# A sparse FFN layer's expert rows: scattered to their places block by block, and loaded plainly at the end

## The chip, the cores and the metric

One core of one Trainium2 chip. The metric is the device time of one execution of the whole program in microseconds (us), the median of several runs. Engines: PE (TensorE), DVE (VectorE), ACT (ScalarE), POOL (GpSimd), SP (SyncE, which issues most DMAs here).

## The reference

The program has four attention layers and four FFN layers over x of 8 batches x 112 tokens x 256. The change lies in the sixth step, a mixture of experts:

```python
logits = CAP * tanh((xn @ wg.T) / CAP)             # xn: normalized x, 896 tokens x 256; 8 experts
probs = softmax(logits)
topk_vals, topk_ids = top_k(probs, 2)
topk_w = topk_vals / sum(topk_vals)
h = gelu(xn @ w1[e].T) * (xn @ w3[e].T)            # 1024 wide, per chosen expert e
out[t] = sum over the 2 choices of topk_w * (h @ w2[e].T)
x = x + tanh(g_ffn[2]) * out
```

With the inputs given, the 1792 choices fall on the eight experts as 318, 226, 200, 56, 234, 127, 338 and 293.

## The kernel before, in words

`sparse_ffn` sorts the 1792 (choice, token) pairs into 21 blocks of 128 slots, each block of one expert. An expert's pairs fill 3, 2, 2, 1, 2, 1, 3 and 3 blocks here, so blocks 0 to 16 hold rows and 17 to 20 are empty; an empty slot counts as token 0 for the gather.

`Assignment` makes the routing: DVE works out choices, counts and the slot of every pair (`vector`, L1870 to L1980); PE turns this into lists of token numbers per block by products with one-hot matrices (`tensor_lists`, L1845, into `psT`), and into the weights of the last two blocks (`tensor_weights`, `psW`). All 896 normalized rows are stored to memory (`rows_dram`, L2090), since indirect DMAs read from there.

Then the blocks k = 0 to 20, each engine running through them in its own written order, tied by semaphores:
- **POOL** `gather(k)` (L2111 to L2118): an indirect DMA fetches the 128 rows of block k into one of two buffers. From k = 2 it waits until PE has transposed block k-2 (`x_turned`). POOL also makes two iota tiles (`spread`, L2132) for the last two blocks.
- **PE** `turn(k)` transposes the rows (L2154). ACT and DVE split them and the weights into high and low parts. `up(k, j)` (L93 to L95) makes half j of both up products; `turn_hidden` (L2177) transposes the gated hidden rows; `down(k)` (L2190) makes the block's output `psY`. A loop pass k issues up(k,0), turn_hidden(2k-1), turn(k+1), up(k,1), down(k-1), turn_hidden(2k).
- **DVE** `move(k)` (L2311) copies `psY` to one of two buffers `ys`; it waits until the store two blocks earlier is done.
- **SP** loads the weights (L2072, L2079), 3 MB a block, through a ring of three blocks, and issues `store(k)` (L2084): 128 rows of `ys` go to `y_dram` in slot order. The store of block k-4 stands in pass k of SP's loop, for blocks 0 to 18.

The last two blocks (LATE = 2) come back another way. Their slots in `y_dram` are filled with zeros early (L2092). ACT copies their outputs to `ys` (`move_late`, L2259), and PE multiplies them by `spread`, a 0/weight matrix of slots by tokens, into four PSUM banks `back`, two batches in each (L2219).

At the end POOL, once all nineteen stores have landed, issues sixteen indirect gathers (L2142), one per batch and choice, that fetch each token's row from its slot. DVE adds both choices with their weights to x (`gathered(b)`, L2318), then the `back` rows (`returned(b)`, L2324), then the statistics for the next layer's norm (L128, L138, L108). DVE's order is gathered(0), gathered(1), and then for each b gathered(b+2), returned(b), statistics of b-1. A barrier and the next layer follow.

Of the kernel before, what the change touches and what calls it, by code (L numbers as in the profile page):

```python
# [5 lines left out]
ALU = mybir.AluOpType  # L6
# [7 lines left out]
P = 128  # L14
# [1713 lines left out]
class Assignment:  # L1728
# [6 lines left out]
    def __init__(self, m, st, xT, wgT, ps, size, blocks, late, gate=6):  # L1735
# [40 lines left out]
        self.slot_index = m.sb("r_slot_index", [T, 2 * B], I32)  # L1776
        self.passed, self.expert_f = m.sb("r_passed", [1, blocks, E - 1]), m.sb("r_expert_f", [1, blocks])
        self.expert = m.sb("r_expert", [1, blocks], I32)
        self.lists = m.sb("r_lists", [T, 2 * B, 2, blocks], BF16)
# [4 lines left out]
        self.psT = ps[:, 256:256 + size // P * 2 * blocks]  # L1784
# [13 lines left out]
    def gpsimd(self, pool):  # L1798
# [14 lines left out]
        pool.memset(self.ones, 1.0).then_inc(s, 1)  # L1813
        pool.memset(self.sel[:, B, :], 0.0).then_inc(s, 1)
# [6 lines left out]
    CONSTS = 13  # L1821
# [23 lines left out]
    def tensor_lists(self, pe):  # L1845

        W = 2 * self.blocks
        for h in range(self.size // P):
            for n in range(2 * B):
                pe.wait_ge(self.s_hot_made, n + 1)  # L1850
                mm = pe.matmul(self.psT[:, h * W:(h + 1) * W], self.hot[:, n, P * h:P * h + P],
                               self.lists[:, n].rearrange("t s k -> t (s k)"), start=(n == 0), stop=(n == 2 * B - 1))
        mm.then_inc(self.s_listed, 1)
# [16 lines left out]
    def vector(self, dve):  # L1870
# [75 lines left out]
        dve.tensor_copy(self.slot_index, self.slot).then_inc(self.s_slot_made, 1)  # L1946
# [9 lines left out]
        stepped(dve.tensor_scalar(self.lists[:, :, 1, :], self.inside, self.t_at, None, ALU.mult))  # L1956
        settle()
# [4 lines left out]
        stepped(dve.tensor_reduce(self.token_f, self.psT.rearrange("p (h s k) -> p h k s", s=2, k=K), AX, ALU.add))  # L1962
# [15 lines left out]
        dve.wait_ge(self.s_weights_listed, 1)  # L1978
        dve.tensor_reduce(self.slot_weight, self.psW.rearrange("p (j h) -> p h j", j=3), AX, ALU.add
# [3 lines left out]
def sparse_ffn(nc, st, xT, io):  # L1983
# [17 lines left out]
    y_dram = nc.dram_tensor("f2_y", (BLOCKS * SIZE, D), F32).ap()  # L2001
    with ExitStack() as ctx:
# [61 lines left out]
        def _(sp):  # L2064
# [17 lines left out]
            def store(k):  # L2082
                sp.wait_ge(y_moved, k + 1)
                sp.dma_start(y_dram[k * SIZE:(k + 1) * SIZE, :], ys[k % 2]).then_inc(y_stored[k % 2], 16)  # L2084

# [5 lines left out]
            sp.wait_ge(zeroed, 1)  # L2091
            sp.dma_start(y_dram[(BLOCKS - LATE) * SIZE:BLOCKS * SIZE, :].rearrange("(h p) d -> p h d", p=P),  # L2092
                         bass.AP(tensor=zeros.tensor, offset=zeros.offset,
                                 ap=[list(zeros.ap[0]), [0, LATE], list(zeros.ap[1])])).then_inc(zeros_stored, 16)
# [3 lines left out]
            for k in range(1, BLOCKS):  # L2098
                e = sp.value_load(routing.expert[0:1, k:k + 1], min_val=0, max_val=E - 1)
                load_up(k, e)  # L2100
                if k > 1:
                    load_down(k - 1, last)
                last = e
                if 3 < k and k - 4 < BLOCKS - LATE:
                    store(k - 4)
            load_down(BLOCKS - 1, last)
            for k in range(BLOCKS - 4, BLOCKS - LATE):
                store(k)

        @block.gpsimd  # L2110
        def _(pool):  # L2111
            def gather(k):
                if k > 1:
# [4 lines left out]
                                        ).then_inc(rows_loaded[k % 2], 16)  # L2118

# [669 lines left out]
```

## Time and profile before

| | us |
|---|---|
| median of 3 runs | 1308.14 |
| lowest, highest | 1308.1, 1309.41 |
| the profiled execution, its own time | 1311.16 |
| its span, first to last instruction | 1309.4 |
| blocks of the sparse layer, from the first up product to the last down product's copy | 804.0 to 1029.6 |

The profiled execution is one execution; all rows below are of it, and their times count from the span's start. "busy" is the time in which an engine works; `PEclk` is the share of TensorE's clock that was granted. `[idle before <-releaser]` is the time for which the engine stood idle ahead of a row and what ended it; "remote" is a semaphore's rise for which the profile has no instruction. PE's rows of one kind are merged, and the ends of matmuls are modelled.

### The profile page before, as it was taken

To read this page: it belongs to the slowest core of one execution; us is meant where nothing else is said; L and a number is where in the kernel's file an instruction comes from. 1 tells how busy PE (TensorE), PEld (TensorE's weight loads), DVE (VectorE), ACT (ScalarE), POOL (GpSimd) and SP (SyncE) were. 2 spreads that over 40 slices of the span, in tenths; PEclk is the share of its full clock that TensorE was granted. 3 is DMA by queue.
4 is the path that set the end of the run, shared out by engine and by line. 5 is a ranking of instruction groups with operands and counts; after the bars stand their busy time and mean duration, and the time that the engine had idled before them with its cause. 6 is when DMAs were issued, how large, how long until landed. Compare 5 with 4: busy or idle time off the path is not lost. (4 is left out here: it accounts for less than half of the span.)

```text
span 1309.4 us, 23700 instructions
## 1 busy us (share of the span) xinstructions
PE 1157.5 (88%) x8549; PEld 880.4 (67%) x8549; DVE 817.3 (62%) x1967; ACT 660.4 (50%) x1536; POOL 513.0 (39%) x527
## 2 busy tenths in 40 slices
PE   3999999999999769658999965999999489999877
PEld 3677777777777436545777754888888367777544
DVE  6665555645544443575778756766665377777686
ACT  3345554445554313225667633665664057766565
POOL 1455554555555200028888772000101341361132
PEclk9999999999999879787999976999999779999997
DMA  6000000000000124030010044999993160000000
GB/s 192 2 12 13 8 6 13 1 13 1 1 1 1 34 76 138 24 96 23 24 46 25 12 133 158 376 377 379 350 343 125 51 191 24 14 14 2 2 8 22
DMA packets 81459, 109.03 MB, mean 83 GB/s; under 512 B 9664, under 2 KB 57168, under 8 KB 81344
## 3 DMA queue, kind: packets, MB, share of 16 engines
q1 hardware_dynamic: 79568, 102.93, 24.4%
q0 software_dynamic: 1776, 4.59, 1.2%
q8 instruction: 70, 1.15, 0.4%
q14 instruction: 45, 0.37, 0.1%
HBM read 102.91 MB, written 4.59 MB: 82 GB/s over the span
## 5 line engine op out<-in xcount | busy, mean ns | idle before, releaser
L907 POOL TENSOR_SCALAR a_arena<-a_arena 112x487 f32<-112x487 f32 x128 | 192.7, 1517 | 176.9 <-DVE a_arena L1124 176.9
L1213 ACT ACTIVATE a_arena<-banks,a_arena 112x487 f32<-112x487 f32 x128 | 84.2, 663 | 192.0 <-DVE a_arena L1118 192.0
L1118 DVE TENSOR_REDUCE a_arena<-banks 112x2 f32<-112x974 f32 x64 | 75.0, 1172 | 101.5 <-PE banks L995 101.5
L397 POOL TENSOR_TENSOR a_arena<-a_arena 112x375 f32<-112x375 f32 x128 | 114.5, 920 | 24.4 <-ACT a_arena L704 24.1
L513 PE MATMUL banks<-ident,a_arena 112*126 112x112 f32 x768 | 106.2, 275 | 12.9 <-POOL a_arena L397 10.7
L513 PEld LDWEIGHTS banks<-ident,a_arena 112*126 112x126 f32 x768 | 77.9, 144 | 47.2 <-issue 27.1
L2060 DVE TENSOR_TENSOR f_up_low<-f_arena,f_up_high 128x1024 fp32r<-128x1024 f32 x80 | 95.7, 1218 | 9.5 <-ACT f_up_high L2232 9.5
L712 ACT COPY a_arena<-banks 126x336 f32<-126x336 f32 x128 | 56.0, 437 | 72.7 <-PE banks L513 72.7
L2232 ACT CAST f_up_high<-f_arena 128x1024 fp32r<-128x1024 f32 x84 | 84.2, 1055 | 8.3 <-DMA f_arena<-in_L_ffn_w1T 7.8
L93 PE MATMUL banks<-a_wv_high,a_kvT_high 128*122 128x512 f32 (+1 forms) x224 | 86.3, 385 | 2.1 <-DVE a_kT_low L1070 2.1
L2116 POOL DMA_INDIRECT f_arena<-f_rows,f_arena x21 | 20.2, 961 | 171.0 <-PE banks L2154 156.7
L93 PE MATMUL banks<-a_kvT_high,a_wk_high 128*128 128x488 f32 (+1 forms) x192 | 82.7, 431 | 4.3 <-DVE a_wk_low L1086 3.1
L2190 PE MATMUL banks<-f_arena 128*128 128x256 f32 x336 | 77.7, 385 | 4.2 <-ACT f_arena L2252 4.2
L704 ACT ACTIVATE a_arena<-a_arena 112x375 f32<-112x375 f32 x128 | 76.9, 605 | 2.8 <-DVE a_arena L620 2.8
L94 PE MATMUL banks<-a_wv_low,a_kvT_high 128*122 128x512 f32 (+1 forms) x224 | 78.0, 348 | 0.0
L95 PE MATMUL banks<-a_wv_high,a_kvT_low 128*122 128x512 f32 (+1 forms) x224 | 77.9, 348 | 0.0
L704 ACT ACTIVATE a_arena<-banks,a_arena 112x375 f32<-112x375 f32 x128 | 72.8, 579 | 9.3 <-DVE a_arena L623 8.7
L2190 PEld LDWEIGHTS banks<-f_arena 128*128 128x128 f32 x336 | 64.9, 193 | 14.3 <-ACT f_arena L2252 4.5
L630 DVE COPY a_arena<-banks 126x336 f32<-126x336 f32 x128 | 64.1, 500 | 13.3 <-PE banks L513 13.3
L95 PE MATMUL banks<-a_kvT_high,a_wk_low 128*128 128x488 f32 (+1 forms) x192 | 72.1, 375 | 0.0
L94 PE MATMUL banks<-a_kvT_low,a_wk_high 128*128 128x488 f32 (+1 forms) x192 | 72.0, 375 | 0.0
L93 PE MATMUL banks<-f_up_high,f_x_high 128*128 128x512 f32 x168 | 70.6, 420 | 0.9 <-DVE f_x_low L2291 0.9
(342 smaller groups left out, 2901.2 us busy)
## 6 DMA issues: line engine op xcount, KB each, us to landing
f_arena<-in_L_ffn_w1T SPq DMA_DIRECT2D x42, 512.0 KB, 8.9
f_arena<-in_L_ffn_w3T SPq DMA_DIRECT2D x42, 512.0 KB, 9.2
f_arena<-in_L_ffn_w2T SPq DMA_DIRECT2D x21, 1024.0 KB
a_arena<-in_ctxT SPq DMA_DIRECT2D x24, 375.0 KB, 5.8
a_arena<-in_ctx SPq DMA_DIRECT2D x16, 375.0 KB
f_y<-f_arena SPq DMA_DIRECT2D x19, 128.0 KB, 8.0
a_arena<-in_L_xattn_Wkv SPq DMA_DIRECT2D x2, 1024.0 KB, 9.9
a_arena<-in_fside_BxSxS SPq DMA_DIRECT2D x8, 164.1 KB, 2.4
```

The costliest lines, as they stand in the source:

```text
L93: pe.matmul(out, sh, mh, start=start, stop=False)
L94: pe.matmul(out, sh, ml, start=False, stop=False)
L95: return pe.matmul(out, sl, mh, start=False, stop=stop)
L397: op = pool.tensor_tensor(z, z, gp[u], ALU.mult)
L513: mm = pe.transpose(psT[s][0:SZ, c * T:(c + 1) * T], prob[n % 4 * 2 + s][:, SZ * c:SZ * c + SZ], ident[0:T, 0:T])
L704: act.activation(prob[n % 4 * 2 + s][:, 0:KEYS], src, ACT.Exp, bias=negmax[:, n % 4, s:s + 1], scale=-1.0 if grouped else 1.0, accum_out=t ...
L907: pool.tensor_scalar(z, z, inv[:, n % 4, s:s + 1], None, ALU.mult).then_inc(p_ready, 1)
L1118: dve.tensor_reduce(negmax[:, n % 4, :], banks[0:T, 0:2, 0:KEYS], AX, ALU.max, negate=True).then_inc(max_ready, 1)
L1213: act.activation(prob[n % PR][s][:, 0:KEYS], banks[0:T, s, 0:KEYS], ACT.Exp, bias=negmax[:, n % 4, s:s + 1], accum_out=total[:, n % 4, s:s ...
L2060: op = eng.tensor_tensor(rest[:, part, :], whole[:, part, :], high[:, part, :].bitcast(F32), ALU.subtract)
L2190: mm = pe.matmul(psY[:, 0:D], hs[k % 2][:, c, :], down_w[k % DOWN][:, c, :], start=(c == 0), stop=(c == IC - 1))
L2232: act.copy(rounded_parts(k, i)[0], raw_part(k, i)).then_inc(w_high, 1)
```

## The change

1. `y_dram` is no longer in slot order. It has 1792 rows, one for each (choice, token), and row 1792 beside them for slots that hold nothing.
2. The list product of the routing has a third part, `lists[:, :, 2, :]`, which tells whether a slot's pair is a second choice. From it and the token number DVE makes `target`, the row of `y_dram` for every slot. `slot_index` goes.
3. Block k's rows are scattered by POOL with an indirect DMA to their targets, in POOL's queue behind gather(k+4), and one scatter waits for the one before. SP's stores go.
4. The zeros of the last two blocks' places are scattered by POOL too: two indirect DMAs, the second waiting for the first, and gather(2) behind both.
5. At the end SP, instead of POOL, fetches: eight plain loads of both choices of a batch.
6. PE's products of the late blocks: all eight of the first, then all eight of the second. Two batches share a bank, so `start` is set for the first of them alone.

```diff
-        self.lists = m.sb("r_lists", [T, 2 * B, 2, blocks], BF16)
+        self.lists = m.sb("r_lists", [T, 2 * B, 3, blocks], BF16)
...
+        pool.memset(self.lists[:, 0:B, 2, :], 0.0).then_inc(s, 1)
...
-        dve.tensor_copy(self.slot_index, self.slot).then_inc(self.s_slot_made, 1)
...
+        stepped(dve.tensor_copy(self.lists[:, B:2 * B, 2, :], self.inside[:, B:2 * B, :]))
...
         dve.wait_ge(self.s_weights_listed, 1)
+        stepped(dve.tensor_scalar(self.empty, self.token_f[:, 0, :], 0.0, 2.0 * R + 1, ALU.is_equal, ALU.mult))
+        stepped(dve.scalar_tensor_tensor(self.place, self.psT[:, 2 * K:3 * K], float(R), self.token_f[:, 0, :],
+                                         ALU.mult, ALU.add))
+        settle()
+        dve.scalar_tensor_tensor(self.target, self.place, -1.0, self.empty, ALU.add, ALU.add
+                                 ).then_inc(self.s_slot_made, 1)
...
-    y_dram = nc.dram_tensor("f2_y", (BLOCKS * SIZE, D), F32).ap()
+    y_dram = nc.dram_tensor("f2_y", (2 * R + 1, D), F32).ap()
...
-            def store(k):
-                sp.wait_ge(y_moved, k + 1)
-                sp.dma_start(y_dram[k * SIZE:(k + 1) * SIZE, :], ys[k % 2]).then_inc(y_stored[k % 2], 16)
...
+            wait_low(sp, BLOCKS - 1, 3)
+            sp.wait_ge(zeros_stored, 16 * LATE)
+            for j in range(2):
+                sp.wait_ge(y_stored[j], 16 * ((BLOCKS - LATE + 1 - j) // 2))
+            for b in range(B):
+                sp.dma_start(got[:, :, b, :], y_dram[0:2 * R, :].rearrange("(k b t) d -> t k b d", k=2, b=B)[:, :, b, :]
+                             ).then_inc(got_loaded[b], 16)
...
+            def store(k):
+                pool.wait_ge(y_moved, k + 1)
+                if k:
+
+                    pool.wait_ge(y_stored[(k - 1) % 2], 16 * ((k - 1) // 2 + 1))
+                pool.indirect_dma_start(y_dram, bass.IndirectOffsetOnAxis(routing.target[:, k:k + 1], 0), ys[k % 2], None
+                                        ).then_inc(y_stored[k % 2], 16)
...
+            pool.wait_ge(routing.s_slot_made, 1)
+            pool.wait_ge(zeroed, 1)
+            for h in range(LATE):
+                if h:
+                    pool.wait_ge(zeros_stored, 16 * h)
+                pool.indirect_dma_start(y_dram, bass.IndirectOffsetOnAxis(
+                    routing.target[:, BLOCKS - LATE + h:BLOCKS - LATE + h + 1], 0), zeros, None).then_inc(zeros_stored, 16)
+            pool.wait_ge(zeros_stored, 16 * LATE)
             for k in range(2, BLOCKS):
                 gather(k)
-            pool.wait_ge(zeros_stored, 16)
-            wait_low(pool, BLOCKS - 1, 3)
-            for j in range(2):
-                pool.wait_ge(y_stored[j], 16 * ((BLOCKS - LATE + 1 - j) // 2))
-            for b in range(B):
-                for k in range(2):
-                    pool.indirect_dma_start(got[:, k, b, :], None, y_dram,
-                                            bass.IndirectOffsetOnAxis(routing.slot_index[:, B * k + b:B * k + b + 1], 0)
-                                            ).then_inc(got_loaded[b], 16)
+                if k > 3:
+                    store(k - 4)
+            for k in range(BLOCKS - 4, BLOCKS - LATE):
+                store(k)
...
-            for b in range(B):
-                for h in range(LATE):
-                    if b == 0:
-                        pe.wait_ge(late_moved, h + 1)
+            for h in range(LATE):
+                pe.wait_ge(late_moved, h + 1)
+                for b in range(B):
                     mm = pe.matmul(back[b // 2][0:T, D * (b % 2):D * (b % 2) + D], spread[:, h, b * T:(b + 1) * T],
-                                   ys[(BLOCKS - LATE + h) % 2], start=(h == 0), stop=(h == LATE - 1))
-                if b % 2:
-                    mm.then_inc(back_ready, 1)
+                                   ys[(BLOCKS - LATE + h) % 2], start=(h == 0 and b % 2 == 0),
+                                   stop=(h == LATE - 1 and b % 2 == 1))
+                    if h == LATE - 1 and b % 2:
+                        mm.then_inc(back_ready, 1)
...
             def gathered(b):
-                dve.wait_ge(got_loaded[b], 32)
+                dve.wait_ge(got_loaded[b], 16)
```

How this moves instructions on POOL, from the first two gathers on. Before (L2116 the block gathers, L2132 the iota tiles, L2142 the gathers at the end):

```order
L2060 TENSOR_TENSOR f_up_low<-f_arena,f_up_high 128x512 x8
L2116 DMA f_arena<-f_rows,f_arena 128x256 x2
L2132 IOTA xT 128x896 x2
L2116 DMA f_arena<-f_rows,f_arena 128x256 x19
L2142 DMA f_arena<-f_y,f_arena 112x256 x16
```

Changed, the same place (L2117 the block gathers, L2148 the zeros, L2126 the scatters):

```order
L2117 DMA f_arena<-f_rows,f_arena 128x256 x2
L2141 IOTA xT 128x896 x2
L2148 DMA f_y<-f_arena 1793x256 x2
L2117 DMA f_arena<-f_rows,f_arena 128x256 x3
L2126 DMA f_y<-f_arena 1793x256
L2117 DMA f_arena<-f_rows,f_arena 128x256
```

The two scatters of zeros stand between the iotas and gather(2); scatters and gathers then take turns, and nothing is left of the sixteen.

On PE, the products of the late blocks at the layer's end, with the semaphores that they wait for. Before (L2190 is the last block's `down`):

```order
L2190 MATMUL banks<-f_arena 128x256 [waits f2_late_moved,f2_down_loaded2,f2_h_moved]
L2190 MATMUL banks<-f_arena 128x256 x7
L2219 MATMUL banks<-f_arena,xT 112x256 [waits f2_late_moved,f2_gated_done,f2_spread_made]
L2219 MATMUL banks<-f_arena,xT 112x256 [waits f2_late_moved]
L2219 MATMUL banks<-f_arena,xT 112x256 x14
```

Changed (L2202 and L2230 are the same lines):

```order
L2202 MATMUL banks<-f_arena 128x256 [waits f2_late_moved,f2_down_loaded2,f2_h_moved]
L2202 MATMUL banks<-f_arena 128x256 x7
L2230 MATMUL banks<-f_arena,xT 112x256 [waits f2_late_moved,f2_gated_done,f2_spread_made]
L2230 MATMUL banks<-f_arena,xT 112x256 x7
L2230 MATMUL banks<-f_arena,xT 112x256 [waits f2_late_moved]
L2230 MATMUL banks<-f_arena,xT 112x256 x7
```

The wait for the second late block has moved from behind one product to behind eight.

## Rows read from the trace of the kernel before

**Rows 1.** The page, part 1: busy time and share of the span by engine

```profile
PE 1157.5 (88%) x8549; PEld 880.4 (67%) x8549; DVE 817.3 (62%) x1967; ACT 660.4 (50%) x1536; POOL 513.0 (39%) x527
```

**Rows 2.** Three stretches; columns as in the first line, in us; engines' instructions as (x)

```profile
core 0: us, PE busy (x) PEld busy (x) DVE busy (x) ACT busy (x) POOL busy (x), PEclk, DMA share, GB/s
804.00:808.00 4.00, 3.96 (x9) 3.14 (x10) 0.00 (x0) 0.83 (x1) 0.81 (x1) 0.50 0.95 283
808.00:812.00 4.00, 4.00 (x21) 3.23 (x20) 2.21 (x4) 2.81 (x5) 0.94 (x1) 0.99 0.95 324
850.00:900.00 50.00, 50.00 (x249) 42.33 (x248) 33.37 (x41) 31.06 (x46) 4.72 (x5) 1.00 1.07 378
```

**Rows 3.** Order of time, layer's end: start us, us, engine line op tiles xcount [idle before]

```profile
1003.74 0.42 DVE L2311 COPY f_arena<-banks 128x256 f32<-128x256 f32 x1 [0.46 <-PE banks L2190]
...
1006.78 0.95 POOL L2142 DMA_INDIRECT f_arena<-f_y,f_arena  x1 [28.26 <-DMA f_y<-f_arena]
...
1007.45 0.58 ACT L2252 COPY f_arena<-banks 128x512 f32<-128x512 f32 x1
...
1009.96 3.62 PE L2190 MATMUL banks<-f_arena 128*128 128x256 f32 x16
...
1013.41 1.04 PE L2177 MATMUL banks<-ident,f_arena 128*128 128x128 f32 x8
...
1015.24 0.58 ACT L2252 COPY f_arena<-banks 128x512 f32<-128x512 f32 x1 [1.25 <-PE banks L2177]
...
1018.04 0.58 ACT L2252 COPY f_arena<-banks 128x512 f32<-128x512 f32 x1 [2.22 <-remote]
...
1018.68 5.41 PE L2190 MATMUL banks<-f_arena 128*128 128x256 f32 x16 [4.24 <-ACT f_arena L2252]
...
1025.25 0.93 POOL L2142 DMA_INDIRECT f_arena<-f_y,f_arena  x1 [0.30 <-issue]
1029.28 0.37 ACT L2259 COPY f_arena<-banks 128x256 f32<-128x256 f32 x1 [10.65 <-remote]
...
1032.64 0.42 DVE L2324 TENSOR_TENSOR x<-banks,x 112x256 f32<-112x256 f32 x1 [15.98 <-PE banks L2219]
...
1042.82 0.17 DVE L108 TENSOR_SCALAR ve<-mv 112x7 f32<-112x7 f32 x1
```

**Rows 4.** Order of time, SP, the store of all rows in the routing

```profile
773.91 0.97 SPq L2090 DMA_DIRECT2D f_rows<-f_arena  x1
```

**Rows 5.** One line's view, L2116, its first two gathers

```profile
DMA to landing us min/median/max: 2.7/2.7/2.7
```

**Rows 6.** Order of time, DVE, part of the routing

```profile
792.61 0.15 DVE L1946 CAST f_arena<-f_arena 112x16 int32<-112x16 f32 x1
...
794.67 0.39 DVE L1956 TENSOR_SCALAR f_arena<-xT,f_arena 112x336 bf16<-112x336 f32 x1
795.10 2.69 DVE L1959 TENSOR_SCALAR f_arena<-f_arena 112x128 bf16<-112x128 bf16 x16
```

**Rows 7.** Order of time, POOL, the gathers for blocks 2, 4 and 5

```profile
803.85 0.96 POOL L2116 DMA_INDIRECT f_arena<-f_rows,f_arena  x1 [0.16 <-issue]
...
816.10 0.94 POOL L2116 DMA_INDIRECT f_arena<-f_rows,f_arena  x1 [5.74 <-PE banks L2154]
826.17 0.94 POOL L2116 DMA_INDIRECT f_arena<-f_rows,f_arena  x1 [9.12 <-PE banks L2154]
```

**Rows 8.** Order of time, PE: row transposes of block 2, first down product

```profile
815.45 0.38 PE L2154 MATMUL banks<-ident,f_arena 128*128 128x128 f32 x2
...
818.41 3.62 PE L2190 MATMUL banks<-f_arena 128*128 128x256 f32 x16
```

**Rows 9.** One line's view, L2116 from 826 us on, sixteen gathers

```profile
DMA to landing us min/median/max: 5.7/6.1/6.6
```

**Rows 10.** One line's view, L2084, the nineteen stores of SP

```profile
DMA to landing us min/median/max: 5.4/8.0/11.5
```

**Rows 11.** One line's view, L2116 at 809 us, the gather for block 3

```profile
DMA to landing us min/median/max: 5.9/5.9/5.9
```

More of the change, by code:

```diff
@@ L1775, in __init__ @@
         self.weights, self.slot_weight = m.sb("r_weights", [T, 2 * B, 3, late], BF16), m.sb("r_slot_weight", [P, late])
-        self.slot_index = m.sb("r_slot_index", [T, 2 * B], I32)
         self.passed, self.expert_f = m.sb("r_passed", [1, blocks, E - 1]), m.sb("r_expert_f", [1, blocks])
         self.expert = m.sb("r_expert", [1, blocks], I32)
-        self.lists = m.sb("r_lists", [T, 2 * B, 2, blocks], BF16)
+        self.lists = m.sb("r_lists", [T, 2 * B, 3, blocks], BF16)
+        self.empty, self.place = m.sb("r_empty", [P, blocks]), m.sb("r_place", [P, blocks])
+        self.target = m.sb("r_target", [P, blocks], I32)
         self.token_f = m.sb("r_token_f", [P, size // P, blocks])
@@ L1783, in __init__ @@
         self.psC = ps[0:T, B * E:2 * B * E + E]
-        self.psT = ps[:, 256:256 + size // P * 2 * blocks]
+        self.psT = ps[:, 256:256 + 3 * blocks]
         self.psW = ps[:, 384:384 + 3 * late]
@@ L1819, in gpsimd @@
         pool.tensor_copy(self.row_b, self.row_at).then_inc(s, 1)
-    CONSTS = 13
+    CONSTS = 14
     def tensor_logits(self, pe):
@@ L1845, in tensor_lists @@
     def tensor_lists(self, pe):
[L1847 to L1852, printed above, removed]
+        for n in range(2 * B):
+            pe.wait_ge(self.s_hot_made, n + 1)
+            mm = pe.matmul(self.psT, self.hot[:, n, 0:P], self.lists[:, n].rearrange("t s k -> t (s k)"),
+                           start=(n == 0), stop=(n == 2 * B - 1))
         mm.then_inc(self.s_listed, 1)
@@ L1961, in vector @@
         dve.wait_ge(self.s_listed, 1)
-        stepped(dve.tensor_reduce(self.token_f, self.psT.rearrange("p (h s k) -> p h k s", s=2, k=K), AX, ALU.add))
+        stepped(dve.tensor_reduce(self.token_f, self.psT[:, 0:2 * K].rearrange("p (h s k) -> p h k s", s=2, k=K), AX, ALU.add))
         settle()
@@ L2090, in _ @@
             sp.dma_start(rows_dram.rearrange("(b t) d -> t b d", b=B), xn).then_inc(x_stored, 16)
[L2091 to L2094, printed above, removed]
             sp.wait_ge(routing.s_expert_made, 1)
@@ L2103, in _ @@
                 last = e
-                if 3 < k and k - 4 < BLOCKS - LATE:
-                    store(k - 4)
             load_down(BLOCKS - 1, last)
-            for k in range(BLOCKS - 4, BLOCKS - LATE):
-                store(k)
+            wait_low(sp, BLOCKS - 1, 3)
[5 more added lines that the diff above has]
+                             ).then_inc(got_loaded[b], 16)
         @block.gpsimd
```

## The prediction

> **What bounds the kernel now.** I read the page first, then the stretches, then the order of time at the two ends of the sparse layer. The page gives TensorE (PE) 88% of the span [rows 1]; the stretches say where that holds. From 808 us on PE is busy 50.00 of 50.00 us at the full clock [rows 2], and a block takes 10.1 us. So inside the blocks nothing on SP, POOL or DVE is worth anything unless it stops PE, and whatever does stop PE there is lost in full. DMA is also near its limit in that stretch (378 GB/s, share 1.07): a transfer of POOL's takes its place beside the weights.
>
> At the end of the layer it is the other way round. The last stretch of `up` is over by 1010; then come short pieces with waits. Read [rows 3]: the sixteen gathers of L2142 are issued one every 1.23 us, 1006.78 to 1026.18. PE's eight transposes are over by its records at 1014.45, yet ACT's copies of them start at 1015.24 and 1018.04; PE's last `down` is over at 1024.09 by its records, yet ACT's copy of it (L2259) starts at 1029.28. The profile calls both releases "remote": the semaphore rose when no matmul record ended. Both late releases, 3.5 us and 5.2 us, lie in the time in which POOL's gathers were under way; the same copies before the gathers (1007.45) follow their transposes at once. The rows do not say why. DVE waits 15.98 us for PE and then works without a gap from 1032.64 to 1042.99, and the layer ends. PE's releases, not the arrival of the rows, set this end: the last gather was issued at 1025.25, over 7 us ahead of DVE's release, and DVE runs through them without a gap.
>
> **The tail, step by step.** The sixteen gathers go. Eight plain loads take their place; SP issues a larger transfer (896 rows) in 0.97 us [rows 4], so eight take under 7.8 us. They start when the scatter of block 18 has landed. Its rows are ready at 1004.16 (L2311), so at 1007 if it lands in the 2.7 us of a gather on a quiet queue [rows 5], at 1011.4 if it takes 7.0. Eight issues and a landing later it is 1022 at worst for the last, and the first three, which DVE wants ahead of PE, are there by 1017. This is hidden behind PE; if it were later than 1023 it would be next in line.
>
> PE: I take it that without gathers the releases follow the records. Transposes end at 1014.45, ACT's two copies run 0.5 us apart from 1014.0 and end at 1015.15, `down` takes the 3.62 us of its predecessor at the full clock instead of 5.41 [rows 3] and ends at 1018.8 instead of 1029.25. Now the new order costs: all eight matmuls of the first late block stand ahead of the second's. Each is as large as one of `down`'s eight, so 3.45 us; then two of the second block and the pipeline, 1.05 us. The first of them starts 0.2 us ahead of `down`'s end, as matmuls overlap, and DVE is released at 1018.6 + 3.45 + 1.05 = 1023.1. Before it was at 1032.64. DVE's chain behind it is unchanged, 10.35 us. **Tail: -9.5 us.** Of this the reorder alone is a loss: from the end of `down` to DVE's release it was 3.4 us, and is 4.3, though at a better clock.
>
> **The front, step by step.** Routing gains a DVE copy of 112x168; the nearest row, 112x336 to bf16, takes 0.39, so 0.3 with its settling; a cast of 112x16 goes, issued 0.07 us ahead of the next; PE's sixteen list matmuls have 63 columns for 42 but follow DVE's sixteen compares (2.69 us) either way [rows 6]. The memset on POOL lies some 9 us before anyone waits for it. The three new DVE instructions on target places end before POOL has finished its gather(1) and the iota. **+0.3 us.**
>
> The large term is on POOL. In its queue the two scatters of zeros, each waited for, now stand ahead of gather(2). Before, gather(2) went at 803.85, right behind the iota [rows 7]. Now: scatter at 803.85, landed after L, 0.27 us from release to issue (turn(2) ends at 815.83, gather(4) goes at 816.10 [rows 7, 8]), second scatter, L, 0.27, gather(2), landed 6.1 us later, which is what a gather takes beside the weights: 5.7 to 6.6 in sixteen of them [rows 9]. That is 810.5 + 2L. PE wants these rows at 815.45, in the middle of block 1, and behind turn(2) stand its up(1,1), and ACT's splits and DVE's low parts of block 2. PE thus stands 2L - 4.96 us.
>
> L is in no row. Its near bounds are the loaded gather, 6.1, same size and queue but reading memory, and the store to the same tensor, median 8.0 [rows 10], which writes memory but queues behind the weights on SP. I take the middle, 7.0. The far bounds are 2.7 (quiet gather) and 11.5 (longest store). A stand of 2 x 7.0 - 4.96 = **9.0 us**. After it the clock: when PE resumed at 804.04 the granted clock was 0.50 up to 808.1 and 0.99 behind it [rows 2]. At 1.2 GHz instead of 2.4 for 4.1 us, **+2.0 us**. Gather(3) and later ones are then issued in time again, since they need only their own turn.
>
> In the blocks, nineteen scatters join nineteen gathers on POOL, 0.95 us of issue each in 10.1 us. Store(k-4) stands in front of gather(k+1) and waits for DVE's copy and for the store before it. But its rows are ready before that gather's own release: `down` of block 0 ends at 822.0 and its copy takes 0.42, so store(0) goes at 822.7; gather(5) went at 826.17 [rows 3, 7, 8]. DVE wants the buffer back two blocks later, 20 us, against an L of 7 to 11.5. SP is rid of a wait and a store a block, but PE was full already. Cost and gain 0, and the cover is large: 3 us on POOL, 9 on the buffer.
>
> **Sum.** +0.3 + 9.0 + 2.0 - 9.5 = +1.8 us. The rows are of an execution of 1311.16 us (span 1309.4); the median of the runs is 1308.14, 3.0 lower. I put the difference on the median: **1309.9 us**. A measurement of this kernel tells about 0.2%, 2.6 us, from no change, so this is "no change", close to slower. With L from 6.1 to 8.0 the same case gives 1308.1 to 1311.9.
>
> **Rivals.**
> - **The scatters land fast.** With L near 2.7, turn(2) waits 0.4 us and the clock stays: 0.3 + 0.4 - 9.5, **1299.3 us**. For it: the weights' traffic only begins at 803.4 and gather(1), issued at 800.99, landed in 2.7. Against: gather(3), issued at 809.42, took 5.9 [rows 11], and all later ones 5.7 or more. The Trainium skill, "DMA: Bandwidth & Descriptors", section "Anatomy of one DMA — SWDGE (gpsimd) path", fits a transfer as 2.0 us plus bytes over 436 GB/s, which for 128 KB is 2.3 us; by that the sum would be about this one. The rows of loaded gathers do not agree with it. Chance 0.17.
> - **The repeated row is slow (slower than before).** For the given inputs blocks 17 to 20 are empty, so both scatters of zeros write 128 rows of 1 KB all to row 1792. If such writes go one behind the other, L rises. It decides from L = 7.4 on, where the sum passes +2.6; at the longest store's 11.5 the stand is 18.0 and the time 1308.14 + 0.3 + 18.0 + 2.0 - 9.5 = **1318.9 us**. Against: gathers of the empty blocks, which all read one row, took no longer than others (5.7 to 6.6). The Trainium skill, same page, section "Rules for kernel authors", says that of a repeated destination each duplicate's write goes out on its own; no row here shows it. Chance 0.13.
> - **The late releases stay.** If what holds back PE's semaphores is not POOL's gathers, the tail keeps them and its slow clock, and the new order adds its 4.3 - 3.4 = 0.9. Then +0.3 + 9.0 + 2.0 + 0.9: **1320.3 us**. Against: before the gathers the copies follow at once. Chance 0.13.
>
> **How the numbers follow.** The forecast case has 0.52: 0.30 of it within 0.2%, 0.19 above, 0.03 below. With the rivals, and 0.05 for things unseen on the slow side: faster 0.20, same 0.30, slower 0.50. The range must take in the fast rival and the slow row, so 1299 to 1319; the last rival is left out. The forecast's own range is 1308.1 to 1311.9.
>
> **What would show it.** In the profile after: two scatters of zeros, the second some 7 us behind the first; PE idle some 9 us ahead of the third pair of row transposes, released by the gather; clock 0.5 in the 4 us behind. PE as full as before from then to 1004 + 11. At the end ACT's L2259 copy follows `down` at once, no "remote", and DVE waits for the late-block matmuls, not for the loads. The forecast falls if the scatters land in under 4 us or over 9, or if a late release stands in the new trace without POOL at work.

## The result, and the profile after

| | before | after |
|---|---|---|
| median of 6 runs each, us | 1308.78 | 1322.94 |
| lowest, highest | 1308.1, 1309.41 | 1314.29, 1325.55 |
| ratio, 95% interval | | 1.0101 [1.0079, 1.0122] |
| profiled execution, own time | 1311.16 | 1321.29 |
| its span | 1309.4 | 1319.7 |

The changed kernel is 1.0% slower. The forecast was "no change", 1309.9 us, with a range up to 1319: too low by 13 us, and the measured time lies outside the range. (The chances had given 0.50 to "slower", for a longer landing or one of the rivals, and not for what is found below.)

I first cut both spans into three parts at two points that both kernels have: SP's first load for the sparse layer, and its first load for the layer behind it. "Ahead", "layer" and "behind" are these three parts in all that follows. Order of time, SP, of the kernel before:

```profile
770.41 0.39 SPq L1796 DMA_DIRECT2D f_arena<-in_L_ffn_wgT  x1
...
1044.73 0.39 SPq L328 DMA_DIRECT2D a_arena<-in_ctxT  x1
```

and of the kernel after:

```profile
775.09 0.38 SPq L1797 DMA_DIRECT2D f_arena<-in_L_ffn_wgT  x1
...
1024.73 3.85 SPq L2108 DMA_DIRECT2D f_arena<-f_y  x8
1051.64 0.40 SPq L328 DMA_DIRECT2D a_arena<-in_ctxT  x1
```

The sparse layer, the only code that the change touches, went from 274.33 to 276.55 us: **+2.2**. The sum of the prediction was +1.8. The layers ahead of it took 770.41 and 775.09 us, +4.7, and what lies behind it 264.7 and 268.0 us, +3.3. So 8.0 of the 10.2 us between the two profiles lie in code that is the same in both kernels. Everything below is about these two findings.

**The front of the layer.** Order of time, POOL, of the kernel after:

```profile
808.62 1.02 POOL L2148 DMA_INDIRECT f_y<-f_arena  x1 [0.17 <-issue]
815.83 1.98 POOL L2148 DMA_INDIRECT f_y<-f_arena  x1 [6.19 <-DMA f_y<-f_arena]
824.37 0.97 POOL L2117 DMA_INDIRECT f_arena<-f_rows,f_arena  x1 [6.55 <-DMA f_y<-f_arena]
825.65 0.96 POOL L2117 DMA_INDIRECT f_arena<-f_rows,f_arena  x1 [0.30 <-issue]
831.03 0.94 POOL L2117 DMA_INDIRECT f_arena<-f_rows,f_arena  x1 [4.42 <-PE banks L2166]
```

The zeros' own line, L2148, their landings:

```profile
DMA to landing us min/median/max: 6.9/7.6/8.3
```

PE's row behind them, and the stretches (columns as in [rows 2]):

```profile
830.07 0.69 PE L2166 MATMUL banks<-ident,f_arena 128*128 128x128 f32 x2 [9.54 <-DMA f_arena<-f_rows,f_arena]
```

```profile
824.00:828.00 4.00, 0.00 (x0) 0.00 (x0) 0.00 (x0) 0.00 (x0) 1.93 (x2) 0.50 1.07 380
828.00:832.00 4.00, 1.93 (x6) 1.64 (x7) 0.42 (x1) 1.21 (x2) 0.94 (x1) 0.50 1.05 374
832.00:836.00 4.00, 4.00 (x16) 3.27 (x15) 2.80 (x3) 2.12 (x4) 0.00 (x0) 0.80 1.09 366
...
850.00:900.00 50.00, 50.00 (x250) 42.34 (x249) 33.37 (x41) 31.53 (x45) 12.98 (x11) 1.00 0.97 342
```

Read it downwards: two scatters, the second waiting for the first, gather(2) waiting for the second, landed 5.7 us later, and PE idle for 9.54 us until then. The granted clock falls to 0.50 in the stand (1.2 of 2.4 GHz), and comes back some 3.5 us after PE has resumed at 830.07: PE's records of the same product take 0.63 us up to 833.11 and 0.39 from 833.81 on, and the stretch 832 to 836 has 0.80. From 850 on PE is as full as in [rows 2]; POOL's 12.98 us for 4.72 are the scatters, and they cost nothing: from the second block's copy to the nineteenth, every one of DVE's copies (L2323) comes 11.60 us later in the layer than before.

**The tail.** Order of time, ACT, PE and DVE, of the kernel after, to be held against [rows 3]:

```profile
1029.90 0.37 ACT L2271 COPY f_arena<-banks 128x256 f32<-128x256 f32 x1 [2.86 <-PE banks L2202]
1030.34 1.07 ACT L2264 COPY f_arena<-banks 128x512 f32<-128x512 f32 x2
1035.22 0.37 ACT L2271 COPY f_arena<-banks 128x256 f32<-128x256 f32 x1 [3.81 <-PE banks L2202]
```

```profile
1029.70 1.04 PE L2189 MATMUL banks<-ident,f_arena 128*128 128x128 f32 x8
1031.46 3.72 PE L2202 MATMUL banks<-f_arena 128*128 128x256 f32 x16 [0.73 <-ACT f_arena L2264]
1035.02 7.07 PE L2230 MATMUL banks<-f_arena,xT 128*112 128x256 f32 x32
```

```profile
1039.54 0.42 DVE L2336 TENSOR_TENSOR x<-banks,x 112x256 f32<-112x256 f32 x1 [8.96 <-PE banks L2230]
...
1049.73 0.17 DVE L108 TENSOR_SCALAR ve<-mv 112x7 f32<-112x7 f32 x1
```

No copy is released by "remote" any more. ACT's last copy follows the end of `down` (1035.18) by 0.04 us, where it took 5.2 before, and `down` takes 3.72 us for 5.41. SP's eight loads are issued in 3.85 us in all and landed after 2.7 to 5.8, in time.

### The profile page after: what moved, and what is told of

The parts are those of the page before. It is cut to its first block and busy times, and to the rows that moved or that the text cites. A ratio compares the mean times of both kernels' runs of the same rounds, so it can differ in the third digit from the quotient of the medians.

```text
span 1319.7 us, 23717 instructions
## 1 busy us (share of the span) xinstructions
PE 1159.4 (88%) x8549; PEld 879.3 (67%) x8549; DVE 818.3 (62%) x1970; ACT 660.6 (50%) x1536; POOL 534.6 (41%) x533
## 5 line engine op out<-in xcount | busy, mean ns | idle before, releaser
L2066 DVE TENSOR_TENSOR f_up_low<-f_arena,f_up_high 128x1024 fp32r<-128x1024 f32 x80 | 95.8, 1219 | 10.2 <-ACT f_up_high L2244 10.2
L2126 POOL DMA_INDIRECT f_y<-f_arena x19 | 32.7, 1723 | 115.6 <-DVE f_arena L2323 115.6
L2202 PE MATMUL banks<-f_arena 128*128 128x256 f32 x336 | 76.0, 379 | 0.7 <-ACT f_arena L2264 0.7
L2202 PEld LDWEIGHTS banks<-f_arena 128*128 128x128 f32 x336 | 63.7, 190 | 10.3 <-ACT f_arena L2264 1.0
```

The lines of the kernel that those rows point to most:

```text
L2066: op = eng.tensor_tensor(rest[:, part, :], whole[:, part, :], high[:, part, :].bitcast(F32), ALU.subtract)
L2202: mm = pe.matmul(psY[:, 0:D], hs[k % 2][:, c, :], down_w[k % DOWN][:, c, :], start=(c == 0), stop=(c == IC - 1))
```

## Experiments

The theory for all of them: the layer is longer by what stands at its front (11.6 us) less what its tail saves (9.4), and the rest of the difference is not made by the change. All runs behind the first comparison were made on three chips, here called the second, third and fourth; each ratio is against runs of the kernel before on the same chip. Times in us; the parts ahead, layer and behind are those of one profile each.

| kernel | ahead | layer | behind | ratio to before, 95% interval |
|---|---|---|---|---|
| before (first profile) | 770.4 | 274.3 | 264.7 | |
| before, fourth chip | 776.4 | 274.5 | 265.0 | 1.0001 [0.9984, 1.0019] |
| after (first profile) | 775.1 | 276.6 | 268.0 | 1.0101 [1.0079, 1.0122] |
| after, second chip | 775.4 | 276.5 | 272.1 | 1.0029 [1.0004, 1.0054] |
| after, fourth chip | 773.9 | 276.0 | 271.9 | 1.0045 [1.0028, 1.0062] |
| zeros later, second chip | 775.1 | 265.3 | 264.2 | 0.9949 [0.9924, 0.9973] |
| zeros later, fourth chip | 770.4 | 265.1 | 272.4 | 0.9936 [0.9911, 0.9961] |
| before with plain loads (experiment 3), second chip | 771.8 | 263.0 | 268.6 | 0.9945 [0.9921, 0.9970] |
| zeros later, old order, third chip | 778.0 | 263.1 | 267.7 | 0.9991 [0.9974, 1.0009] |
| zeros later, old order, fourth chip | 773.9 | 262.8 | 267.6 | 0.9936 [0.9916, 0.9957] |
| zeros later + 16 unused gathers, second chip | 774.7 | 272.7 | 267.2 | 1.0026 [1.0002, 1.0049] |
| after, empty slots on rows of their own, third chip | 768.9 | 274.9 | 264.3 | one run |
| zeros later + 6 unused gathers, started later, third chip | 771.2 | 265.2 | 272.4 | one run |
| zeros later + 16 unused gathers, started later, third chip | 769.0 | 272.6 | 268.8 | one run |

The part behind takes values in three groups over these fourteen profiles: 264.2 to 265.0, 267.2 to 268.8 and 271.9 to 272.4 us. One and the same kernel can fall in the first and in the third ("zeros later").

### 1. The changed kernel again, on another chip

No edit.

> The changed kernel once more, beside the kernel before. Theory A (the sparse layer is only about 2 us longer, 11.4 us lost at its front, 9.4 won at its end; the rest of the 14 us lies in unchanged layers and goes with the granted clock of TensorE): times spread over some 10 us again and go down as the mean granted clock of the run goes up; in the profile the sparse layer (from its first weight load to the next layer's first load) is 2 to 3 us longer than the 274 us of before, whatever the total. Theory B (the change makes something in the layer slow in a way that varies): the sparse layer itself differs from the first profile of the changed kernel by several us.

Measured: layer 276.45 us; medians 1318.73 (12 runs) against 1316.9 (35 runs of the kernel before), ratio 1.0029. The layer repeats to 0.1 us. The ratio does not: here the difference of the medians is 1.8 us, not 14. As expected, a run's time goes with its mean granted clock: the fastest of the twelve (1313.91) has 0.936, the slowest (1327.18) 0.926.

### 2. Zeros scattered behind gather(3) and gather(4)

```diff
-            for h in range(LATE):
-                ...
-            pool.wait_ge(zeros_stored, 16 * LATE)
             for k in range(2, BLOCKS):
                 gather(k)
+                ...
+                if 3 <= k < 3 + LATE:
+                    h = k - 3
+                    if h:
+                        pool.wait_ge(zeros_stored, 16 * h)
+                    pool.indirect_dma_start(y_dram, ... zeros, None).then_inc(zeros_stored, 16)
                 if k > 3:
+                    if k == 4:
+                        pool.wait_ge(zeros_stored, 16 * LATE)
                     store(k - 4)
```

> The changed kernel with the two scatters of zeros behind the gathers of blocks 3 and 4 instead of ahead of that of block 2. If the front's loss is the third gather standing behind them: PE no longer waits 9.5 us for turn(2), the granted clock stays 1.0, and the profile's sparse layer is 11.4 us shorter than in the changed kernel, some 263 us; the time falls by about 11 us. Rival (weights' traffic with scatters and gathers in it is what delays block 2, wherever the zeros stand): PE still waits several us in blocks 1 to 3.

Order of time, POOL, of this kernel:

```profile
808.62 0.96 POOL L2117 DMA_INDIRECT f_arena<-f_rows,f_arena  x1 [0.16 <-issue]
814.39 0.94 POOL L2117 DMA_INDIRECT f_arena<-f_rows,f_arena  x1 [4.80 <-PE banks L2170]
815.64 1.01 POOL L2152 DMA_INDIRECT f_y<-f_arena  x1 [0.30 <-issue]
821.08 1.30 POOL L2117 DMA_INDIRECT f_arena<-f_rows,f_arena  x1 [4.43 <-PE banks L2170]
823.30 3.09 POOL L2152 DMA_INDIRECT f_y<-f_arena  x1 [0.92 <-DMA f_y<-f_arena]
832.86 1.80 POOL L2126 DMA_INDIRECT f_y<-f_arena  x1 [6.47 <-DMA f_y<-f_arena]
```

The same two scatters, but gather(2) ahead of them, right behind the iota; PE no longer stands for it. The layer takes 265.25 us, 11.3 less than in the changed kernel: the whole front term, stand and clock together. (276.55 less the 11.4 of the expectation is 265.2; its "some 263" is a slip.) The zeros themselves cost at most 0.2 us where nothing stands behind them that PE is about to need: DVE's copies of the blocks lie 0.30 us later in the layer than before, 0.1 of it the routing. The program is faster than both kernels, by 0.5% against before.

### 3. The kernel before, with eight plain loads on SP

```diff
-            for b in range(B):
-                for k in range(2):
-                    pool.indirect_dma_start(got[:, k, b, :], None, y_dram, ...)
...
+            for b in range(B):
+                sp.dma_start(got[:, :, b, :], y_dram[0:2 * R, :]. ... [:, :, b, :]).then_inc(got_loaded[b], 16)
```

Rows are fetched in slot order, so each token gets other rows than its own; the work is the same in size.

> The kernel before, but the sixteen gathers at the end are eight plain loads of SP from the same tensor, of rows 0 to 1791 in slot order (so rows come to wrong tokens); all else, the order of PE's late products too, is as before. Theory A (POOL's gathers hold back PE's semaphores): no release by remote, ACT's late copy follows the last down product at once, the end of the layer is 10.4 us earlier (9.5 and the 0.9 that the new order costs). Rival (the late releases have another cause, such as the clock or the late copies themselves): they stay, and the time is within 2 us of before.

The layer takes 263.03 us, 11.3 less than before (10.4 was expected), and no release at the layer's end is "remote". So the gathers' removal alone, with SP's stores and the old order of the late products kept, is worth 11.3 us. The 9.4 of the changed kernel is that less about 2 for the new order (experiment 7).

### 4. The gathers put back where nobody needs them

Experiment 2's kernel, and sixteen gathers of rows that nothing reads, on POOL behind its last scatter; POOL waits for them at the end.

```diff
+            wait_low(pool, BLOCKS - 1, 3)
+            for n in range(2 * B):
+                ...
+                pool.indirect_dma_start(spare, None, rows_dram, ...).then_inc(extra_loaded, 16)
+            pool.wait_ge(extra_loaded, 16 * 2 * B)
```

> The zeros-later kernel with sixteen indirect gathers added on POOL behind its last scatter, of normalized rows into a part of SBUF that nobody reads. They run beside PE's last transposes and products, as the gathers of before did. Theory A: the releases by remote come back, ACT's copies of the last transposes and of the last down product start some us behind PE's records, and the layer is up to 9 us longer than in the zeros-later kernel. Rival (it takes the gathers from the tensor just stored, or DVE reading what they bring): no late release, and the end of the layer waits at most for POOL's last gather.

Order of time, ACT and POOL, of this kernel:

```profile
1020.96 0.58 ACT L2276 COPY f_arena<-banks 128x512 f32<-128x512 f32 x1 [1.79 <-remote]
1022.39 0.58 ACT L2276 COPY f_arena<-banks 128x512 f32<-128x512 f32 x1 [0.85 <-remote]
1033.71 0.37 ACT L2283 COPY f_arena<-banks 128x256 f32<-128x256 f32 x1 [10.73 <-remote]
```

```profile
1017.30 1.18 POOL L2165 DMA_INDIRECT f_arena<-f_rows,f_arena  x1 [0.30 <-issue]
...
1029.86 0.93 POOL L2165 DMA_INDIRECT f_arena<-f_rows,f_arena  x1 [0.30 <-issue]
```

The late releases are back: the two groups of transposes end at 1018.66 and 1019.11 and are copied at 1020.96 and 1022.39, `down` ends at 1029.24 and is copied at 1033.71, 4.5 us late. PE's instructions are those of experiment 2 and nothing reads the gathered rows. DVE's release (1035.29) lies 7.4 us later in the layer than in experiment 2, and that is by how much the layer is longer. The medians on this chip, 1319.32 and 1307.97, differ in the same direction. POOL's gathers hold back PE's semaphores, and no data dependence does. When the first of the late transposes end, six gathers have been issued (the sixth starts at 1017.30). The release of `down` comes 1.2 us after POOL's wait for the last gather is over (1032.51).

### 5. Six and sixteen gathers, started later

The same, but POOL first waits for `move_late` of the first late block, so that the gathers start 8.4 us before DVE's release; once six of them, once sixteen.

> The extra-gathers kernel with six extra gathers instead of sixteen, and they start when ACT has copied the first late block (late_moved), as the last transposes run. In both kernels with late releases the first late one came when six gathers had been issued, 1.23 us apart. Theory C (a backlog: gathers issued faster than something drains them, PE's semaphores late from the sixth on): no late release at the last down product, which ends some 5 us after the first gather; if any, small ones at the end. Theory D (any gather of POOL in flight holds back PE's semaphores): the release of the transposes and of the last down product come late by a us or more, as with sixteen.

> As the six-gathers kernel, with all sixteen, from late_moved on. Theory C (backlog): the releases of the transposes and of the last down product are prompt, and those of the late-block products, which run when six or more gathers have been issued, come late by several us and hold DVE back. Theory D (any gather in flight): the transposes and down are late too.

With six: layer 265.17, as without gathers, and nothing "remote". With sixteen the layer takes 272.60, yet again nothing is "remote": from the first late product to DVE's release it is 4.52 us, as in experiment 2 (4.51), with seven gathers issued by then. The trace also has the rise of the semaphore for all four banks of late products, at 1021.97, 1022.83, 1023.69 and 1024.56, each within 0.02 us of its product's end, and by the last of them nine gathers have been issued. So the late releases that this kernel's expectation named for a backlog did not come. What is longer here is something else, the last rows of POOL:

```profile
1032.19 0.93 POOL L2166 DMA_INDIRECT f_arena<-f_rows,f_arena  x1 [0.30 <-issue]
1041.56 0.10 POOL L400 MEMSET a_arena<- 128x1 f32 x1 [8.44 <-POOLq L84]
```

The last gather lands at 1034.86 and POOL's wait for it ends at 1034.88; then POOL's `DRAIN`, the instruction that closes its part of the layer, takes 4.80 us, and the next layer starts behind it, while DVE was done at 1032.4. In the kernel of experiment 4 the same `DRAIN` took 4.80 us too, but ended (1037.5) while DVE still worked.

So the number of gathers issued does not decide by itself: six were enough for a late release in experiment 4, nine held back nothing here. The two kernels differ in where the train starts: right behind the last scatter there, 8.2 us later in the layer here. Why that matters, and by what path POOL's gathers reach PE's semaphores, stays open. What is shown is that the sixteen at their place in experiment 4 make both releases late, and that they are prompt without them.

### 6. Zeros of the late blocks to distinct rows

The changed kernel, with `empty` adding 1793 + partition in place of 1793, so that an empty slot's target is a row of its own beside the 1792.

> The changed kernel, but the empty slots of a scatter go to 128 rows of their own (1792 plus the slot's partition) instead of all to row 1792. If the repeated row makes the scatters slow: the two scatters of zeros land in about the 6.1 us of a gather instead of 6.9 and 8.3, the scatter of block 18, which has only empty slots, lands in under 3 us instead of 3.9, and PE's wait for turn(2) falls from 9.5 to 7 us. If it is writing through POOL's queue beside the weights as such: landings and the wait stay within 1 us of the changed kernel's.

The list of waits, 800 to 840 us, and POOL's order of time:

```profile
PE banks L2168 <- DMA f_arena<-f_rows,f_arena: 8.8, 2, 6.9
```

```profile
802.45 1.02 POOL L2150 DMA_INDIRECT f_y<-f_arena  x1 [0.17 <-issue]
808.23 0.98 POOL L2150 DMA_INDIRECT f_y<-f_arena  x1 [4.76 <-DMA f_y<-f_arena]
814.74 1.22 POOL L2119 DMA_INDIRECT f_arena<-f_rows,f_arena  x1 [5.53 <-DMA f_y<-f_arena]
```

From the first scatter to gather(2) it is 12.29 us for 15.75, and PE stands 6.9 us for 9.5. The layer is only 1.6 us shorter: behind this stand PE's products run at the lower clock for 5.7 us (821.0 to 826.7), where it was 3.5 in the first profile of the changed kernel. That kernel's other two profiles give the spread: PE's stand 8.65 and 8.78 us, its scatters 6.6 and 7.0 us for the first and 7.5 for the second. So the rival of the repeated row was in part true: the repeated row costs 1.1 to 2.0 us a scatter, against a single profile of distinct rows. What is left, 5.5 and 6.3 us for the two scatters, is what a loaded gather takes. By the Trainium skill ("DMA: Bandwidth & Descriptors", section "Rules for kernel authors") each duplicate's write of a repeated destination goes out on its own; the section gives no time for it, and the direction measured here agrees.

### 7. The old order of the late products

Experiment 2's kernel with PE's products batch by batch, as before.

```diff
-            for h in range(LATE):
-                pe.wait_ge(late_moved, h + 1)
-                for b in range(B):
+            for b in range(B):
+                for h in range(LATE):
+                    if b == 0:
+                        pe.wait_ge(late_moved, h + 1)
...
```

> The zeros-later kernel with PE's late products in the order of before (both blocks for one batch, then the next). My working says that the new order costs: eight products of the first late block ahead of the second, 4.3 us from the end of down to DVE's release (4.50 from its last record in the changed kernel), against about 2.1 us in the old order at the full clock. So the profile's sparse layer is some 2 us shorter than the 265.25 of the zeros-later kernel. Rival (the new order keeps PE busy, and what is won by the order is lost by a lower granted clock behind the gap): same layer within 0.5 us, granted clock lower in the last 10 us.

> The zeros later and the old order of the late products, a second time, with a profile of the kernel before from the same chip beside it. Theory: layer 263.1 us, 11.2 less than before, and the time is lower than the kernel before by 11 us less what the unchanged layers give back through the clock; the first comparison found none of it (0.9991), so the parts ahead and behind must be longer here by some 5 to 11 us, with more time at 1.2 GHz. Rival (the chip's own executions differ that much, and the first comparison was one of them): the parts ahead and behind are as long as in the kernel before within 2 us, and the ratio is about 0.992.

DVE's release, of the kernel on the third chip:

```profile
1029.02 0.42 DVE L2340 TENSOR_TENSOR x<-banks,x 112x256 f32<-112x256 f32 x1 [6.67 <-PE banks L2235]
```

`down` ended at 1026.97 there, so DVE goes 2.05 us behind it, where the new order takes 4.36 (1035.18 to 1039.54 above). The layer is 263.1 and 262.8 us long, for 265.3 and 265.1 with the new order: the reorder costs 2.2 to 2.3 us on both chips. On the fourth chip this kernel is 0.64% faster than before (medians 1308.63 and 1317.41, 8.8 us, of 11.8 that the layers differ by). Of the two profiles there the parts ahead and behind add up to the same in both kernels, to 0.2 us, so the rival of the second expectation holds on this chip. On the third chip it is the same as before (1308.07 and 1308.10), though its layer is as short.

### 8. Before, after, and both versions of experiment 2 on one chip

> The kernel before, unchanged, profiled a second time, on the same chip as the three runs behind it. Theory (the layer's length is fixed by its own waits, and what differs between the executions besides lies in the unchanged layers with the granted clock): the sparse layer takes 274.3 us, within 0.6, with both late releases at its end, and the parts ahead of it and behind it differ from the first profile's 770.4 and 264.7 by up to 5 us, with more time at 1.2 GHz where they are longer. Rival (the late releases came by chance in the one profile read, and the layer of the kernel before is as a rule shorter, which would be why the kernel with the zeros later and the old order of products gained nothing on the second chip): the layer takes 263 to 268 us and has no late release.

> The changed kernel, unchanged, on one chip with the three others. Theory: the layer takes 276.5 us, within 0.6, as in its two profiles, which is 2.2 us more than before; the difference of the medians is 2.2 us and whatever the clock of the unchanged layers adds, between 0 and 14. Rival (the change slows the layers it does not touch by some 8 us in every execution): the parts ahead and behind are together at least 6 us longer than those of the kernel before on this chip.

> The zeros later with the new order of the late products, on the same chip as the old order. Theory: layer 265.3 us, 2.2 more than with the old order. The difference of the two medians says whether such a step of the layer reaches the program's time at all: 2 us if it does, anything between -5 and +5 if the unchanged layers' clock covers it.

The second profile of the kernel before settles what the first could not. Its layer takes 274.54 us, with both late releases, 0.2 off the first. But the same instructions ahead of the layer take 776.4 us for 770.4. Stretches, first profile of before, then the second, then the first of the changed kernel:

```profile
400.00:440.00 40.00, 35.81 (x286) 27.05 (x287) 16.51 (x34) 16.97 (x42) 20.99 (x14) 0.96 0.00 1
440.00:460.00 20.00, 14.79 (x70) 7.95 (x70) 9.41 (x19) 5.43 (x7) 0.65 (x1) 0.91 0.30 56
...
480.00:500.00 20.00, 15.81 (x57) 9.86 (x58) 6.63 (x15) 4.78 (x9) 0.00 (x0) 0.82 0.64 185
```

```profile
400.00:440.00 40.00, 35.81 (x285) 27.02 (x282) 16.51 (x34) 16.97 (x42) 20.48 (x14) 0.95 0.00 1
440.00:460.00 20.00, 14.90 (x53) 7.59 (x53) 9.13 (x19) 3.62 (x5) 0.65 (x1) 0.68 0.29 55
...
480.00:500.00 20.00, 13.53 (x46) 9.31 (x47) 7.58 (x18) 1.65 (x3) 1.45 (x2) 0.66 0.58 161
```

```profile
440.00:460.00 20.00, 14.91 (x58) 7.07 (x56) 9.16 (x19) 4.51 (x5) 0.65 (x1) 0.74 0.29 55
480.00:500.00 20.00, 14.79 (x50) 9.89 (x51) 7.65 (x18) 1.88 (x4) 0.55 (x1) 0.69 0.63 178
```

Up to 440 the first two are alike. Then PE is busy for as long in both (14.8 and 14.9 of 20 us) but is granted 0.68 of its clock for 0.91, and 0.66 for 0.82 later. The same instructions of DVE come 0.5 us earlier at 400, 1.1 us later at 443, 4.2 at 488 and 6.1 at 577, and the difference stays at about 6 up to the sparse layer. It comes from there, not from an edit. The 4.7 us ahead of the layer in the first pair come from the same place: in the changed kernel, granted 0.74 and 0.69 there, DVE's instructions come 0.3 us earlier than before at 443, about 3 later at 488 and 4.7 later at 700.

The part behind the layer differs as much within one kernel: 264.2 and 272.4 us for "zeros later", with a granted clock of 0.92 and 0.89. The whole part behind, the run on the second chip, then on the fourth:

```profile
1040.34:1304.54 264.20, 231.01 (x2098) 166.24 (x2098) 193.75 (x407) 167.89 (x439) 82.28 (x98) 0.92 0.12 36
```

```profile
1035.41:1307.85 272.44, 236.33 (x2098) 169.66 (x2098) 194.32 (x407) 168.05 (x439) 82.16 (x98) 0.89 0.12 35
```

The changed kernel on this chip: layer 275.95, 1.4 us over before, and a median 5.6 us over it. The rival of a change that slows the layers it does not touch by at least 6 us fails on this pair (ahead 773.9 for 776.4, behind 271.9 for 265.0, together +4.4), but 4 us stay over that the layer does not account for. The two orders of experiment 7, 2.3 us apart in the layer, have medians of 1308.63 and 1308.85: on six and eight runs such a step drowns in the rest.

## Why the prediction was wrong

| term | predicted | measured, first profiles |
|---|---|---|
| routing | +0.3 | +0.1 (first scatter 33.53 us into the layer; gather(2) 33.44 before) |
| PE's stand | +9.0 | +9.8 to 9.9, of it 9.54 idle |
| clock behind it | +2.0 | +1.7 |
| blocks | 0 | 0 |
| tail | -9.5 | -9.4 |
| sum, sparse layer | +1.8 | +2.2 |

**The steps of the sum held.** L was taken as 7.0 us; the two scatters took 6.9 and 8.3. By the formula that is a stand of 10.2, less 0.4 because gather(2) landed in 5.7 and not 6.1. The shift of ACT's work behind the stand is 9.9 (816.17 to 830.79, less the 4.69 that the layer starts later), and 1.7 more by the last block's copy (1003.74 to 1020.03). The clock term is a little under the 2.0 because PE ran 3.5 us at the lower clock and not 4.1. Two things in this agreement are luck. L came out near 7.0 as the middle of a gather and a store, but it is a loaded write of 5.5 to 6.3 us and the cost of the repeated row, which the forecast had set aside as a rival. And stand and clock scatter: the whole front took 11.6, 11.5 and 11.0 us in the changed kernel's three profiles, against the first of before. The tail came from where it was said to: both late releases went, `down` is back to 3.7, and from `down`'s end to DVE it is 4.36 us for the predicted 4.3; DVE's chain is unchanged. The rival that the late releases stay is refuted. The rival of fast scatters fell too: no scatter of the changed kernel landed in under 3.9 us. The Trainium skill ("DMA: Bandwidth & Descriptors", section "Anatomy of one DMA — SWDGE (gpsimd) path") fits 2.0 us plus bytes over 436 GB/s, an estimate of 2.3 us for 128 KB; the trace does not agree beside the weights, with 6.9 and 8.3.

**The step that failed is the last: "I put the difference on the median."** It took for granted that all the rest of the program, 1035 of 1309 us, takes the same time in both kernels. In the first pair of profiles it took 8.0 us longer, for +2.2 in the layer, and the medians are 14.2 apart. The experiments show two things about this remainder. It is not fixed for a kernel: the kernel before had medians of 1308.8, 1308.1, 1316.9 and 1317.4 us in four sets of runs, and its two profiles differ by 6.0 us ahead of the sparse layer and by 0.2 in it. And it goes with the granted clock in layers where PE is idle at times: 0.68 for 0.91 over 440 to 460 us, where 2.5 of the 6.0 us arise, and 0.89 for 0.92 where the part behind is 8.2 us longer. In the first comparison the kernel before ran at its lower level and the changed one at its upper (1322.9, 1318.7 and 1323.0 in three sets). The median was forecast as one number where I should have held such a remainder against a second profile; the range was built from terms of the layer alone and had no term for it. Only the 4.7 us ahead of the layer are traced to such a stretch; for the rest of the miss the place is shown, outside the layer, and the cause is not.

**What stays open.** In each of the three sets the changed kernel was slower by more than its layer or by about as much: 14.2, 1.8 and 5.6 us, against 1.4 to 2.2. Its part behind the layer was 268.0, 272.1 and 271.9, that of before 264.7 and 265.0. Whether the later end of the layer leads the clock into the longer case more often there, or chance did in five profiles, isn't settled: other kernels show both lengths, the kernel before with plain loads 268.6 among them. Nor is it settled why the shortest layers gained 8.8 us on one chip and nothing on another, for which there is no profile of before.

One thing was missing in the argument on the tail, without harm to the sum: I gave the reorder a cost of 0.9 us, from 3.4 to 4.3. The 3.4 was measured while the clock was down behind the late release (0.50 over 1028 to 1032). At full clock the old order takes 2.05, and the reorder costs 2.2 to 2.3. Without it, and with the zeros later, the layer is 11.5 us shorter than before: at its best 1308.6 against 1317.4.

## What to carry to other kernels

Ask of everything that is put into a queue what already stands there and who waits for it: the scatters of zeros cost at most 0.2 us behind gather(3) and gather(4), and 11.3 us more ahead of gather(2). Cut a change's effect out of the profile between two fixed points around the code it touches, for both kernels, before believing a difference of medians; and profile the kernel before twice, since only that shows what the untouched code does by itself. When a change saves something by ending a stall, price its other parts at the clock that holds without the stall.

## What the runs showed of the hardware

- A train of sixteen indirect gathers from POOL, one each 1.23 us, held back semaphores of PE that have nothing to do with them: those of the last transposes by 1.2 to 3.7 us, with six gathers issued when the first of them ended, and that of the last `down` by 4.4 to 5.2. Started 8.2 us later in the layer, a train held back none with up to nine issued; what decides is open.
- POOL's `DRAIN` at the layer's end took 4.80 us behind sixteen such gathers that had all landed, and 3.98 behind six.
- A scatter of 128 rows to one and the same row took 6.6 to 7.0 us and, as the second, 7.5 to 8.3, where one to distinct rows took 5.5 and 6.3. POOL's issue of the second took 1.98 us in one profile and 3.09 in experiment 2, but 0.99 and 0.98 in two further profiles of the changed kernel, the same as with distinct rows; so the repeated row does not explain the long issues.
- A scatter of a block's rows takes 1.72 us of POOL's time to issue in the changed kernel, where a gather takes 0.95; the forecast had counted 0.95. It was covered.
- The same code took 770.4 and 776.4 us in two executions of one kernel, and 2.5 us of the difference arise in 20 us where the granted clock was 0.91 in the one and 0.68 in the other.
